# Attention values products issued in runs of four key tiles instead of two

## The reference

```
sh_a, sc_a, gt_a, sh_m, sc_m, gt_m = split(silu(cond) @ Wada + bada, 6)
xm = layernorm(x, g1, be1) * (1 + sc_a) + sh_a
q, k, v = heads(xm @ Wqkv)
attn = softmax(where(causal, q @ k.T * 32**-0.5, -inf))
x = x + gt_a * ((attn @ v) @ Wproj + bproj)
xm = layernorm(x, g2, be2) * (1 + sc_m) + sh_m
x = x + gt_m * (gelu(xm @ W1 + b1) @ W2 + b2)
```

## Time and profile before

| | us |
|---|---|
| median of three runs | 3668.57 |
| lowest and highest of the three | 3665.08, 3668.9 |
| the profiled execution | 3666.15 |
| its span, first to last instruction | 3664.4 |
| what lies around the span | 1.75 |
| PE busy in the span | 3489.2 (95%) |
| DVE, ACT, POOL busy | 1622.4, 1202.4, 1009.2 |
| mean granted TensorE clock | 0.984 of full |

### The profile page before, as it was taken

How to read it: one execution, slowest core, us unless ns; L and a number is a source line. 1 busy time by engine, 2 the same in 40 slices (tenths; PEclk the granted TensorE clock), 3 DMA queues, 4 the chain that set the end, 5 groups by cost and what they waited for, 6 DMA issues and landing times.

```text
span 3664.4 us, 60630 instructions
## 1 busy us (share of the span) xinstructions
PE 3489.2 (95%) x20076; PEld 2470.1 (67%) x20076; DVE 1622.4 (44%) x2130; ACT 1202.4 (33%) x2578; POOL 1009.2 (28%) x1267
## 2 busy tenths in 40 slices
PE   6889999999999999999884999999999999999999
PEld 3655555555555555553332889998999989999998
DVE  3344544444444444444443444444444444444442
ACT  1134444445444544444552111111111111111111
POOL 1212222222222222222223333332333333333332
PEclk8889999999999999999997999999999999999999
DMA  5435554454554544545444222122212222122220
GB/s 197 140 123 157 149 159 143 146 157 139 156 157 147 154 148 147 161 125 162 136 114 112 60 70 64 53 68 55 69 54 64 55 68 66 51 69 54 69 57 13
DMA packets 227210, 392.79 MB, mean 107 GB/s; under 512 B 30160, under 2 KB 96720, under 8 KB 227080
## 3 DMA queue, kind: packets, MB, share of 16 engines
q1 hardware_dynamic: 213648, 369.42, 35.2%
q10 hardware_dynamic: 13440, 22.03, 1.7%
HBM read 271.71 MB, written 119.11 MB: 107 GB/s over the span
## 4 chain that ended last, share of the span: by engine, by line
PE 91%; ACT 3%; DVE 2%; issue 2%; DMA 1%; POOL 0%; ACTq 0%; SPq 0%; DVEq 0%; POOLq 0%
PE psH L728 20%; PE psY L741 19%; PE psA L640 15%; PE psA L580 10%; PE psT L617 10%; PE psP L707 5%; PE psA L576 5%; PE psS L595 4%; PE psS L599 2%; ACT e L810 2%; DVE mx L1031 1%; PE psP L717 1%; ACT xm_full L788 1%; PE psT L540 1%; PE psA L559 1%
## 5 line engine op out<-in xcount | busy, mean ns | idle before, releaser
L1031 DVE TENSOR_REDUCE mx<-psS 128x4 f32<-128x2048 f32 (+3 forms) x384 | 675.6, 1759 | 867.1 <-PE psS L599 587.4
L810 ACT ACTIVATE e<-psT 128x512 f32<-128x512 f32 (+3 forms) x1536 | 680.4, 492 | 849.9 <-PE psT L617 825.3
L1257 POOL TENSOR_TENSOR h_l<-h_full,h_h 128x256 fp32r<-128x256 f32 x512 | 488.4, 954 | 1121.4 <-DVE h_h L1180 1121.4
L910 ACT ACTIVATE h_full<-psH,b1c 128x256 f32<-128x256 f32 x512 | 243.9, 476 | 1332.4 <-PE psH L728 1332.4
L728 PE MATMUL psH<-a_h,w1p_h 128*128 128x256 f32 x2048 | 577.9, 282 | 7.5 <-DVE a_l L1175 7.5
L728 PE MATMUL psH<-a_h,w1p_l 128*128 128x256 f32 x2048 | 580.4, 283 | 0.0
L728 PE MATMUL psH<-a_l,w1p_h 128*128 128x256 f32 x2048 | 579.9, 283 | 0.0
L640 PE MATMUL psA<-e,vst 128*33 128x512 f32 (+3 forms) x3072 | 570.0, 492 | 0.8 <-POOL e L1283 0.2
L617 PE MATMUL psT<-qst,kst 97*128 97x512 f32 (+3 forms) x1536 | 513.4, 394 | 47.1 <-ACT e L810 43.5
L1180 DVE CAST h_h<-h_full 128x256 fp32r<-128x256 f32 x512 | 150.1, 293 | 899.7 <-ACT h_full L910 899.7
L1283 POOL TENSOR_SCALAR_AFFINE_SELECT e<-e 128x256 f32<-128x256 f32 x512 | 219.4, 429 | 1142.2 <-ACT e L810 1142.2
(11 more groups left out here) (100 smaller groups left out, 3917.2 us busy)
## 6 DMA issues: line engine op xcount, KB each, us to landing
qk_split<-qk_hl SPq DMA_DIRECT2D x128, 512.0 KB, 3.2
kst<-qk_split SPq DMA_DIRECT2D x128, 256.0 KB, 4.0
qst<-qk_split SPq DMA_DIRECT2D x128, 256.0 KB, 4.2
values<-vaug ACTq DMA_DIRECT2D x64, 264.0 KB, 2.1
vst<-values SPq DMA_DIRECT2D x32, 528.0 KB, 3.9
attended<-o_sb SPq DMA_DIRECT2D x256, 66.0 KB
xin<-in_x_dram SPq DMA_DIRECT2D x64, 256.0 KB, 3.8
kmx<-qk_split SPq DMA_DIRECT2D x32, 512.0 KB, 4.3
```

What stands on the lines that cost most here:

```text
L810: act.activation(e[:, s % ERING, hd, 0:w], psT[:, hd, 0:w], ACT.Exp, scale=SCALE)\
L910: act.activation(h_full[:, m % 4, :], psH[:, m % 4, 0:RA], ACT.Gelu, bias=b1c[:, m:m + 1])\
L1031: dve.tensor_reduce(mx[:, part, :, qt], psS[:, :, 0:w], AX_X, ALU.max).then_inc(sem("max_reduced"), 1)
L1257: return pool.tensor_tensor(dst, full, high.bitcast(F32), ALU.subtract)
```

## The change

`RUN = 4` key tiles of both heads are multiplied in one run, sixteen machine matmuls, every fourth step, instead of two key tiles in every second step. The run of chunks s - 5 to s - 2 is issued in steps 1 mod 4, where the run of chunks s - 3 and s - 2 stood; steps 3 mod 4 have none. The last four chunks of all are done after the last pass.

```diff
+RUN = 4
@@ values
-                if c in (0, 4):
-                    wait(pe, sem("o_copied"), g * 2 + c // 4)
+                if c in (0, RUN):
+                    wait(pe, sem("o_copied"), g * 2 + c // RUN)
                 if c in DIAG:
-                    pe.wait_ge(sem("masked"), g * len(DIAG) + DIAG.index(c) + 2)
+                    pe.wait_ge(sem("masked"), g * len(DIAG) + DIAG.index(c) + RUN)
                 else:
-                    pe.wait_ge(sem("exp_done"), (u * BODY_STEPS + s) * 2 + 4)
+                    pe.wait_ge(sem("exp_done"), (u * BODY_STEPS + s + RUN) * 2)
                 past(pe, "pe")
-                for d in range(2):
+                for d in range(RUN):
@@ body
-                    if s % 2 == 1 and not (isinstance(u, int) and u == 0 and s == 1):
-                        values(u, s - 3)
+                    if s % RUN == 1 and not (isinstance(u, int) and u == 0 and s == 1):
+                        values(u, s - RUN - 1)
@@ after the last pass
-            values(NU - 1, BODY_STEPS - 2)
+            values(NU - 1, BODY_STEPS - RUN)
```

## The result

| | before | after |
|---|---|---|
| median, us | 3668.74 (4 runs) | 3783.23 (4 runs) |
| lowest to highest | 3665.08 to 3669.43 | 3780.15 to 3794.83 |
| profiled execution | 3666.15 | 3780.15 |
| mean granted clock | 0.984 | 0.959 |

The ratio is 1.032, with a 95% interval of 1.0303 to 1.0338. I had predicted 3677 and a range that ended at 3687. The sign was right, the size was wrong by a factor of thirteen.

A forecast was written before the change was run, and what follows sets the result against it. TensorE's queue was taken to bound the filled passes. Passes 0 to 12 gave +0.9 us, 13 and 14 +4.6, 15 +3.2: +8.7 on 3666.15, 3674.9; plus 2.4 for the median, 3677. Range 3663 to 3687.

The forecast's parts named there:

- What bounds the kernel now: Passes 1 to 11: TensorE busy 1217.41 of 1238.00 us at full granted clock, so its queue sets the time.
- the rivals: Switch from maxima to scores dear (3684 us, 0.20), cheap (3669, 0.18) or cheaper still (3661, 0.08); or no effect (3668, 0.04).
- What becomes late: Waits for VectorE no longer hidden by removed runs: 2.1 us a pass in passes 13 and 14, less in filled passes.
- The maxima: Row maxima at least 2.90 us apart for VectorE's reduction: filled passes wait +0.29 us behind step 11, +0.28 behind step 31.
- The 1.62 us that I took off for step 15: Filled passes, step 15: 4.88 us between maxima less 1.62 for leaving columns is 3.26, so no wait.
- The turned maxima: Steps 19 and 43: transpose to maxima takes 0.64 us without the run hiding VectorE's copy, +0.31 us twice a pass.
- What a run costs: Each removed run saves TensorE 0.12 us behind unmasked maxima (range 0.03 to 0.23), 0.25 behind masked ones, steps 23 and 47.
- cheaper still: Rival, chance 0.08: maxima to run hides a drain of some 0.1 us that scores don't pay; 3661 us.
- The 0.1 us for a late copy at step 3: Filled passes: an item beginning at step 3 finds ScalarE's last copy barely late, 0.1 us once a pass.
- Passes 13 to 15 besides: Last three passes: exposed weight pieces, 0.5 us each in 13 and 14; in 15, +1.2 at step 19, +1.0 at the end.
- How the numbers follow: Chances for the whole kernel: forecast 0.50; slower 0.49, same 0.43, faster 0.08, with bounds 3661 and 3676 us.
- My sign of being wrong: Filled passes changing by over 0.7 us each would mean the switch from maxima to scores was not as taken.

The follow-up runs named there:

- e5_warm: Changed kernel plus eight small extra matmuls, output unused, at the end of each step without a values run in passes 13 to 15: 3735.63 us.
- e6_keep43: Kernel before, with every step 3 mod 4 but 43 joined to the next run in passes 0 to 12 only: 3685.84 us.
- e8_waits: Kernel before, with every step 3 mod 4 but 43 and 47 joined to the next run in passes 0 to 12 only: 3670.93 us.
- e4_free: Kernel before, with only steps 3, 7, 15, 23, 27, 35 and 39 joined to the next run in passes 0 to 12: 3655.84 us.
- e10_turned: e4_free with steps 11 and 31 joined too, and the values run put ahead of the maxima in steps 13 and 33: 3649.14 us.
- e7_keep47: Kernel before, with every step 3 mod 4 but 47 joined to the next run in passes 0 to 12 only: 3712.04 us.
- e11_fill43: e7_keep47 plus twelve small extra matmuls, output unused, in step 43 of passes 0 to 12: 3676.99 us.

## Why the prediction was wrong

Step by step, by its own parts:

- **What bounds the kernel now.** The sentence "at full granted clock" was a reading of the earlier trace rows, and it was used as a constant. This is the step that failed. The sum has no term for the clock and the rivals have none; I had the lengths of the steps without a run nearly right and didn't ask what three of them in a row do. Of the 114.0 us, at least 49.5 in passes 13 to 15 are the clock's (e5_warm). In the looped filled passes: a pass at full clock with step 43 kept is +1.6 over before (e6_keep43), step 43 adds 0.5 (if it costs what step 19 does in e8_waits), and measured are +4.1 on average (116.73 less 112.65), so 2.0 a pass are the clock's, about 26 us over thirteen passes as an estimate.
- **What becomes late.** ScalarE's loop turn was missed; the sum has no term for it. The trace of before has it, 2.48 us from the branch at 1008.99 to the next instruction, but only in its records of branches: it lies within an idle time that ends with TensorE's scores and is as long without a turn. I listed who waits for VectorE and never asked what stood under the run in step 47. Price 1.7 us, ten times: 17 us.
- **The maxima.** Right: 2.90 us from maxima to maxima was measured as 2.90 and 2.91; +0.29 and +0.28 were 0.31 and 0.31. (The 1.62 us that I took off for step 15 is not its columns, which are 1.50; there is no wait either way.)
- **The turned maxima.** Right in kind, 0.31 was 0.50. The transpose to the maxima takes 1028.27 - 1027.43 = 0.84 us in the changed kernel, not 0.64: the copy ends at 1028.02, so the 0.05 us I gave the signal are 0.25. TensorE and VectorE in step 43 of pass 6, changed kernel:

```profile
1027.43 0.27 PE L606 MATMUL psS<-ident,mxc 128*32 128x128 f32 x1
1028.27 0.33 PE L596 MATMUL psS<-kmx,qmx 32*128 32x128 f32 x4 [0.56 <-DVE m_row L1044]
```

```profile
1027.74 0.28 DVE L1044 CAST m_row<-psS 32x128 fp32r<-32x128 f32 x1 [3.28 <-PE psS L606]
```

- **What a run costs.** Right: the value I took for maxima straight to scores, between 0.03 and 0.23, was 0.12, and the steps of e4_free give 0.13; with masks 0.24 against 0.25. The rule of the Trainium skill, TensorEngine Tiling (Array Packing), section Key Properties, that a change of the tiling mode drains TensorE, taken at its full price as I did there, would have given 0.23. The 0.13 doesn't bear that price out: the change that stays costs the scores behind it as much as the one that went. The 0.03 us that spoke for the rival "cheaper still" is in no row. The 0.1 us for a late copy at step 3 doesn't exist: that pair of steps saves 0.11.
- **Passes 13 to 15 besides.** At full clock, but for 3.4 us in pass 15 (e5_warm), they come out 3.7, 3.7 and 5.8 us over before, with the extra matmuls in them, against +2.3, +2.3 and +3.2. How much of the difference is the extra work isn't separated.
- **How the numbers follow.** The range reached as far as the costs I had listed. My sign of being wrong came true, +4.1 us in a filled pass where I had set 0.7, but it named the switch from maxima to scores, which was as I took it. A resource that is constant in the trace of before belongs in it as a case when the change takes work out of a stretch.

The order of the parts in the filled passes, then: 26 us clock (the estimate above), 17 us loop turns, and the remaining 5 us of 48 for waits less savings. The saving that the change was about is real and came out in e4_free and e10_turned, where only those runs are joined under which nothing else had been hiding, or where the order was turned to hide it again.

## What to carry over

Moving work out of a step also moves the cover from everything beneath it: list each wait that ended under it, on every engine, including the turns of loops, before counting what is saved. TensorE's clock is one of the things that a steady spread of work keeps up; a change that bunches the same work can halve it in the gaps, and the bunch then pays at 1.2 GHz. Joining only the runs whose cover nobody needed, and in two places putting the cover back, turned a loss of 3.2% into a gain of 0.5%.

## What the runs showed of the hardware

- The granted clock fell to half behind a stretch in which TensorE was busy 4.62 of 5.60 us (changed kernel, pass 13), and behind one with 2.97 of 4.40 us (e7_keep47), with no idle time over 0.66 us in either. The same place with 3.58 of 4.40 us busy kept it (e11_fill43), in eleven of twelve passes (pass 12 had 3.4 us of half clock).
- Behind the branch of ScalarE's first loop come 2.43 to 2.68 us without an instruction, in the kernel before and the changed one, and a transfer of 8192 bytes of the kind "instruction" starts 0.92 to 0.97 us after each of these branches. Behind the one branch of its second loop the next instruction comes after 0.26 us, without such a transfer. In the changed kernel passes 1 and 12 to 15 don't have the pause.
- Scores start as slowly behind four 32-row products side by side as behind narrow values products: the pair takes 0.58 us (e10_turned) and 0.57, against 0.47 behind a full product.
